# Attention blocks of 512 queries in units of two heads, with a shared bank for the block sums

## The chip, the cores and the metric

One core of one Trainium2 chip runs the whole program. The metric is the device time of one execution in microseconds (us); lower is better. The kernel before takes 1469.5 us, the median of three runs (1467.96 to 1470.09).

The engines are named as in the profile: PE is TensorE's matmul stream and PEld its weight loads, DVE is VectorE, ACT is ScalarE, POOL is GpSimd, SP starts DMAs.

## What is computed

Three layers run over x of 8 batches, 1024 tokens, 256 channels. Cut to what matters here:

```python
x = x + linear_attention(group_norm(x))      # 8 heads of 32, layer norm on q and k
t = tokens(x)
t = t + softmax_attention(layer_norm(t))     # 8 heads of 32, 1024 keys per query, then w_agg and b_agg
t = t + experts(layer_norm(t))               # Sinkhorn gates over 8 experts, top 128 tokens each, scatter back
```

The change touches the softmax attention: per batch and head, `exp(q k^T / sqrt(32))`, its sum over keys, its product with v, and the quotient.

## The kernel before, in words

Heads come in two groups (g) of four. A **unit** is one key tile of 128 keys against 256 queries for the four heads of a group. Its four score products (L894, 96 rows by 256 columns each) fill one of two score tiles `score_ps`, one ACT instruction (L1209) writes the exponentials of 128 x 1024 scores into one of four `probs` buffers, and `weigh` (L916) multiplies them by v into the lower half of the PSUM bank `acc`, each head on 32 output partitions of its own, so that the four heads run at the same time. Eight units (kt = 0 to 7) make a **block**: 256 queries of one group. A **slot** is two units; a batch has 32 slots, a block has four.

The sum over keys is split. For kt 1 to 5, DVE adds the exponentials to `prob_sum` (`add_up`, L1635), in 128 x 512 instructions, two for a unit; the first of a block adds units 0 and 1. For kt 6 and 7 PE adds them with a matrix of ones (L913) into the upper half of `acc`, and `total` (L926) adds `prob_sum` in the same way. At the end of a block ACT copies `acc` to `acc_sb` (L1199), DVE inverts the sums (`invert`, L1609) and POOL multiplies (`divide`, L1242); the result, `attn_T`, is what `agg` multiplies by w_agg.

Everything else is a list of **steps** (`order`), dealt over the slots of a batch: while batch b is in softmax attention, the front of batch b+1 (`xT`, `x_stats`, `gmean`, `gvar`, `xn`, `qk0`, `v0`, `dots`, `lin`, `zT`, `proj`, `v`, `norms`) and the store of batch b-1 (`agg`, `store_stats`, `store_rows`, `z2T`, `gate`) are worked off between the units. A `rest` in the list leaves slots empty. Within a slot every engine goes, in its own program order, through: the score products or exponentials of the next slot, the first half of the slot's steps, `weigh` or `add_up` of this slot, the second half. No engine reorders, so an instruction that waits holds all that stands behind it on its engine. PE writes the products of steps into three `shared` banks in turn, and each must be read by ACT or DVE before its next use.

Two waits matter: the score products of a unit wait until the tile's last exponentials are done (`exp_done`), and the exponentials wait until their buffer's last content has been weighed (`weighed`) and added up (`summed`). So DVE may be about one slot behind before ACT stops, and ACT about one slot before PE stops.

The routing of the experts (Sinkhorn, selection, gathers and scatters) is spread over the last three batches and a tail without attention.

## Time and profile before

| | us |
|---|---|
| median of three runs | 1469.5 |
| profiled execution, its span | 1467.7 |
| PE busy | 1339.3 (91%) |
| DVE busy | 1021.3 (70%) |
| ACT busy | 868.7 (59%) |
| POOL busy | 562.6 (38%) |

The span is the profiled execution from its first to its last instruction; the median of the runs is 1.8 us above it. Busy times are unions of an engine's records. Matmuls are pipelined, so the length of one record is more than what it costs in a stream: the distance from one start to the next is the price.

### The profile page before, as it was taken

Reading aid. Unit: us, or ns where it says so; the run is one execution under the profiler, and the core shown is the slowest. Engines: PE = TensorE matmul, PEld = TensorE weight load, DVE = VectorE, ACT = ScalarE, POOL = GpSimd, SP = SyncE. Lnnn points to the kernel's source line nnn. Section 1 sums busy time; section 2 is a strip of 40 time slices with the busy share of each in tenths; the row PEclk is TensorE's granted clock in tenths of the full one; section 3 lists DMA queues with packets and bytes.
Section 4 is the critical chain, followed back from the end, with each engine's and each line's share of the span. In section 5 each row is a group of like instructions: output and inputs, shape, how many; then the busy total and the mean of one; then the engine's idle time right before and its main releaser. Section 6 shows DMA issues by size and latency. Waiting matters only on the chain.

```text
span 1467.7 us, 29142 instructions
## 1 busy us (share of the span) xinstructions
PE 1339.3 (91%) x10849; PEld 915.8 (62%) x10849; DVE 1021.3 (70%) x2114; ACT 868.7 (59%) x1268; POOL 562.6 (38%) x1068
## 2 busy tenths in 40 slices
PE   5789989999999999999999999999998999987535
PEld 3556656667576767676767676656666567766423
DVE  3536766858585857586768676787789776899771
ACT  2456557677667767677666767665675667542100
POOL 1132530445134513551245214520554116875443
PEclk9899989999999999999999999999999999999665
DMA  2051013600360037002710272005500265454322
GB/s 79 29 137 51 1 30 87 172 16 27 80 184 15 2 93 193 18 2 75 184 46 2 57 168 79 2 30 117 144 15 2 65 169 191 128 158 134 118 68 80
DMA packets 66785, 119.13 MB, mean 81 GB/s; under 512 B 10705, under 2 KB 46546, under 8 KB 66642
## 3 DMA queue, kind: packets, MB, share of 16 engines
q1 hardware_dynamic: 57682, 90.48, 22.9%
q0 software_dynamic: 8960, 26.75, 6.0%
q8 instruction: 89, 1.46, 0.4%
q14 instruction: 54, 0.44, 0.1%
HBM read 29.11 MB, written 33.55 MB: 43 GB/s over the span
## 4 chain that ended last, share of the span: by engine, by line
PE 62%; DVE 24%; issue 6%; POOL 4%; ACT 3%; DMA 0%; DVEq 0%; POOLq 0%; ACTq 0%
PE shared L938 30%; PE scores L894 12%; PE acc L916 11%; DVE prob_sum L1635 6%; PE acc L913 3%; PE shared L933 3%; DVE acc_sb L1609 2%; DVE bn L1344 2%; ACT probs L1209 2%; DVE work L1543 1%; PE acc L926 1%; DVE resid L1350 1%; DVE best_i L1541 1%; DVE best L1539 1%; DVE bn_x L1404 1%
## 5 line engine op out<-in xcount | busy, mean ns | idle before, releaser
L1209 ACT ACTIVATE probs<-scores 128x1024 f32<-128x1024 f32 x512 | 516.0, 1024 | 178.1 <-PE scores L894 94.0
L894 PE MATMUL scores<-query_stack,key_stack 96*128 96x256 f32 x2048 | 342.1, 308 | 16.0 <-ACT probs L1209 15.7
L1635 DVE TENSOR_TENSOR prob_sum<-prob_sum,probs 128x512 f32<-128x512 f32 x512 | 331.3, 707 | 0.0
L894 PEld LDWEIGHTS scores<-query_stack,key_stack 96*128 96x128 f32 x2048 | 275.9, 192 | 85.1 <-issue 39.1
L916 PE MATMUL acc<-probs,v_all 128*32 128x256 f32 x4096 | 289.2, 389 | 0.0
L1242 POOL TENSOR_TENSOR attn_T<-acc_sb 128x256 f32<-128x256 f32 x56 | 41.4, 740 | 447.8 <-DVE acc_sb L1609 445.0
L938 PE MATMUL shared<-w_sb,chan 128*128 128x512 f32 (+1 forms) x512 | 186.7, 501 | 5.9 <-DVE chan L1438 5.9
L916 PEld LDWEIGHTS acc<-probs,v_all 128*32 128x32 f32 x4096 | 114.8, 110 | 104.0 <-issue 37.9
L938 PEld LDWEIGHTS shared<-w_sb,chan 128*128 128x128 f32 x512 | 91.9, 192 | 62.5 <-issue 57.9
L938 PE MATMUL shared<-chan,w1T 128*128 128x512 f32 x256 | 121.3, 608 | 2.1 <-ACT chan L1125 2.1
L1635 DVE TENSOR_TENSOR prob_sum<-probs 128x512 f32<-128x512 f32 x128 | 98.4, 810 | 18.8 <-ACT probs L1209 16.5
L1609 DVE RECIPROCAL acc_sb<-acc_sb 128x256 f32<-128x256 f32 x64 | 111.4, 1740 | 0.0
L1494 DVE TENSOR_TENSOR lo<-shared,hi 128x512 fp32r<-128x512 f32 x64 | 43.4, 684 | 97.2 <-ACT hi L1162 97.2
L1453 DVE TENSOR_REDUCE ss<-v_all 128x16 f32<-128x512 f32 x64 | 43.8, 685 | 77.6 <-ACT v_all L1139 77.3
L913 PE MATMUL acc<-probs,ones 128*32 128x256 f32 x1024 | 83.0, 397 | 0.0
L1132 ACT ACTIVATE lo<-shared 128x512 f32<-128x512 f32 x64 | 38.1, 595 | 70.8 <-PE shared L938 70.4
L938 PEld LDWEIGHTS shared<-chan,w1T 128*128 128x128 f32 x256 | 46.8, 193 | 50.5 <-issue 49.8
L1499 DVE TENSOR_REDUCE norm_max<-shared 128x1 f32<-128x512 f32 x64 | 43.5, 681 | 39.1 <-PE shared L938 39.1
L1162 ACT ACTIVATE hi<-shared 128x512 fp32r<-128x512 f32 x64 | 37.5, 595 | 51.8 <-PE shared L938 51.5
L787 POOL TENSOR_TENSOR lo<-lo,hr 128x512 f32<-128x512 f32 x46 | 57.1, 1264 | 20.3 <-DVE hr L1371 19.1
L938 PE MATMUL shared<-waggT,attn_T 128*128 128x256 f32 x248 | 61.7, 383 | 1.1 <-DVE attn_T L1619 1.1
L938 PE MATMUL shared<-w1T,chan 128*128 128x256 f32 x256 | 61.2, 384 | 0.0
(220 smaller groups left out, 2036.7 us busy)
## 6 DMA issues: line engine op xcount, KB each, us to landing
query_stack<-hi SPq DMA_DIRECT2D x120, 128.0 KB, 2.5
key_stack<-hi SPq DMA_DIRECT2D x120, 128.0 KB, 2.5
x_sb<-in_x_dram SPq DMA_DIRECT2D x8, 1024.0 KB, 5.3
out_dram<-resid SPq DMA_DIRECT2D x16, 512.0 KB, 4.8
tokens_scratch<-resid SPq DMA_DIRECT2D x16, 512.0 KB, 5.5
tokens_scratch<-rows SPq DMA_DIRECT2D x16, 512.0 KB, 3.3
key_stack<-lo SPq DMA_DIRECT2D x60, 128.0 KB, 2.5
query_stack<-lo SPq DMA_DIRECT2D x60, 128.0 KB, 2.5
```

Of the source, the lines that this page charges most:

```text
L787: last = eng.tensor_tensor(view, view, hr[:, t, :].unsqueeze(2).to_broadcast([P, 2 * H, DH]), ALU.mult)
L894: last = pe.matmul(score_ps[u % 2][:, QB * r:QB * (r + 1)], key_stack[stack, HG * g + r, P * kt:P * (kt + 1)], query_stack[stack, HG * g + ...
L913: pe.matmul(acc[DH * r:DH * (r + 1), QB:2 * QB], ones[:, 0:DH], p[:, QB * r:QB * (r + 1)], start=False, stop=False, skip_group_check=True, ...
L916: last = pe.matmul(acc[DH * r:DH * (r + 1), 0:QB], v_all[:, g, kt, DH * r:DH * (r + 1)], p[:, QB * r:QB * (r + 1)], start=kt == 0, stop=kt ...
L933: last = pe.transpose(ps[:, P * j:P * (j + 1)], m, ident[:, :])
L938: last = pe.matmul(out, stationary, moving, start=j == 0, stop=j == len(pairs) - 1)
L1209: act.activation(probs[:, u % PROBS, :], score_ps[u % 2][:, :], ACT.Exp, scale=DH ** -0.5) \
L1453: dve.tensor_reduce(ss[:, t, :], squares[:, t % 2, :].rearrange("p (h d) -> p h d", d=DH), AX.X, ALU.add).then_inc(s["squares_summed"], 1)
L1494: read(dve.tensor_tensor(lo[:, j, part].bitcast(F32R), ps[:, :], hi[:, j, part], ALU.subtract), seg, *st)
L1499: read(dve.tensor_reduce(norm_max[:, seg.front, j, h:h + 1], ps[:, :], AX.X, ALU.max), seg, *st)
L1609: dve.reciprocal(acc_sb[:, QB:2 * QB], acc_sb[:, QB:2 * QB]).then_inc(s["recip_ready"], 1)
L1635: dve.tensor_tensor(total[:, part], probs[:, (u - 1) % PROBS, part] if kt == 1 else total[:, part], probs[:, u % PROBS, part], ALU.add).th ...
```

## The change

QB becomes 512, so a unit is one key tile against 512 queries for **two** heads (`pair` 0 or 1), and a slot is one key tile with both pairs. A block is 512 queries of one group and has eight slots (one for each kt); a batch has four blocks and still 32 slots.

- Score products: 2 per unit over 512 columns, where there were 4 over 256. One exponential instruction still has 128 x 1024 elements.
- `weigh` and the products with ones go over 512 columns, with half as many instructions. `acc` is now full with the weighed values, so the sums go to one of the three shared banks (`bank_uses` takes it at kt 6 after the first half of the slot, and holds it until the end of kt 7). `total` stands in the slot of kt 6.
- The exponentials of kt 0 are written straight into `prob_sum`; DVE adds kt 1 to 5, two 128 x 1024 instructions for a slot, in five slots in succession. The adds of kt 1 wait for the weighing of kt 0, the exponentials of kt 0 wait for `total` of the block before.
- `copy_acc` is two ACT copies of 128 x 512 per block, of which there are half as many, `invert` is two reciprocals of 128 x 256 and stands between the halves of the slot of kt 0, no longer at its end; `divide` is two multiplications.
- In `order`, `x_stats` and `gmean` come earlier, `agg` 4 to 7 later, since their tokens belong to the last block of the batch.
- The descriptor space of the software DMA queue is set to 8192 bytes.

```diff
-QB = 256
+QB = 512
...
-             ("store_stats", 0), ("xT", 1, 1), ("xT", 0, 0), ("agg", 4), ("agg", 5), ("x_stats",), ("agg", 6),
-             ("store_rows", 0), ("rest", 1), ("agg", 7), ("gmean",), ("store_rows", 1), ("store_rows", 2),
-             ("gvar",), ("store_stats", 1), ("z2T", 0), ("store_rows", 3), ("z2T", 1), ("z2T", 2), ("z2T", 3),
+             ("store_stats", 0), ("xT", 1, 1), ("xT", 0, 0), ("x_stats",), ("store_rows", 0), ("gmean",),
+             ("store_rows", 1), ("rest", 0.5), ("agg", 4), ("agg", 5), ("agg", 6), ("gvar",), ("agg", 7),
+             ("store_rows", 2), ("store_stats", 1), ("z2T", 0), ("store_rows", 3), ("z2T", 1), ("z2T", 2), ("z2T", 3),
...
+            if kt == T - DIRECT and not second:
+                held = take((None, ("total", slot.pair // BLOCK_SLOTS)), banks)
+        if kt == T - 1:
+            held = None
...
+        return probs[:, (2 * ((T - 1) * (k // T) + kt - 1) + pair) % PROBS, :] if kt else prob_sum[:, pair, :]
...
-                for r in range(HG):
-                    last = pe.matmul(score_ps[u % 2][:, QB * r:QB * (r + 1)],
-                                     key_stack[stack, HG * g + r, P * kt:P * (kt + 1)],
-                                     query_stack[stack, HG * g + r, QB * qb:QB * (qb + 1)], start=True, stop=True)
+                for r in range(UNIT_HEADS):
+                    h = HG * g + UNIT_HEADS * pair + r
+                    last = pe.matmul(score_ps[pair][:, QB * r:QB * (r + 1)], key_stack[stack, h, P * kt:P * (kt + 1)],
+                                     query_stack[stack, h, QB * qb:QB * (qb + 1)], start=True, stop=True)
...
-                    weigh(2 * k)
-                    weigh(2 * k + 1)
-                    if k % BLOCK_PAIRS == BLOCK_PAIRS - 1:
-                        total(k // BLOCK_PAIRS)
+                    weigh(k)
+                    if k % T == added + 1:
+                        total(k // T)
...
+                if k % T == 0:
+                    await_count(act, "totalled", k // T)
+                else:
+                    n = before_in_buffer(k)
+                    if n >= 0:
+                        act.wait_ge(s["weighed"], n + 1)
+                    if n >= 0 and n % T <= added:
+                        act.wait_ge(s["summed"], 2 * (added * (n // T) + n % T - 1) + pair + 1)
...
+            def add_up(k, pair):
+
+                kt, total = k % T, prob_sum[:, pair, :]
+                dve.wait_ge(s["exp_done"], 2 * k + pair + 1)
+                if kt == 1:
+                    dve.wait_ge(s["weighed"], k)
+                else:
+                    dve.wait_ge(s["summed"], 2 * (added * (k // T) + kt - 2) + pair + 1)
+                dve.tensor_tensor(total, total, unit_probs(k, pair), ALU.add).then_inc(s["summed"], 1)
...
-                if k is not None:
-                    if k % BLOCK_PAIRS < BLOCK_PAIRS - 1:
-                        add_up(2 * k)
-                    add_up(2 * k + 1)
+                if k is not None and 1 <= k % T <= added:
+                    add_up(k, 0)
+                    add_up(k, 1)
+                elif k and k % T == 0:
+                    invert(k // T - 1)
                 for st in second:
                     step(*st)
-                if k and k % BLOCK_PAIRS == 0:
-                    invert(k // BLOCK_PAIRS - 1)
```

How the instructions stand at the head of a full batch, first on PE. The group statistics of the next batch (`gmean`, the product of `gn_mean` and `small`) wait for DVE's `mean_ready`. Before, all eight `agg` steps (two products each, `waggT,attn_T`) have gone ahead of it; these rows are of slot 3:

```order
L894 MATMUL scores<-query_stack,key_stack 128x256 [waits exp_done]
L894 MATMUL scores<-query_stack,key_stack 128x256 x3
L894 MATMUL scores<-query_stack,key_stack 128x256 [waits exp_done]
L894 MATMUL scores<-query_stack,key_stack 128x256 x3
L938 MATMUL shared<-waggT,attn_T 128x256 [waits attn_ready,read1]
L938 MATMUL shared<-waggT,attn_T 128x256
L938 MATMUL shared<-small,gn_mean 128x2 [waits mean_ready,read2]
L913 MATMUL acc<-probs,ones 32x256 [waits exp_done]
```

In the changed kernel it stands in slot 1, with `agg` 0 to 3 ahead of it, and the score products for slot 3 and then `agg` 4 to 7 behind it:

```order
L969 MATMUL shared<-ident,x_sb 128x128 [waits x_loaded,read2]
L969 MATMUL shared<-ident,x_sb 128x128 x3
L952 MATMUL acc<-probs,v_all 32x512 [waits exp_done]
L952 MATMUL acc<-probs,v_all 32x512 x3
L974 MATMUL shared<-small,gn_mean 128x2 [waits mean_ready,read0]
L922 MATMUL scores<-query_stack,key_stack 128x512 [waits exp_done]
L922 MATMUL scores<-query_stack,key_stack 128x512
L922 MATMUL scores<-query_stack,key_stack 128x512 [waits exp_done]
L922 MATMUL scores<-query_stack,key_stack 128x512
L974 MATMUL shared<-waggT,attn_T 128x256 [waits attn_ready,read1]
```

`gmean` has moved forward past `agg` 4 to 7, from slot 3 to slot 1.

On DVE, the way to `mean_ready` (the COPY into `small`, step `x_stats`) in the kernel before, from directly behind the one reciprocal of slot 0 (`acc_sb<-acc_sb`) on:

```order
L1350 TENSOR_TENSOR resid<-shared,resid 128x256
L1344 BN_STATS bn<-resid 128x6
L1350 TENSOR_TENSOR resid<-shared,resid 128x256
L1344 BN_STATS bn<-resid 128x6 x2
L1362 BN_AGGR mv<-bn 128x2 x4
L1404 BN_STATS bn_x<-chan 128x6
L1635 TENSOR_TENSOR prob_sum<-prob_sum,probs 128x512 x4
L1404 BN_STATS bn_x<-chan 128x6
L1350 TENSOR_TENSOR resid<-shared,resid 128x256 x2
L1344 BN_STATS bn<-resid 128x6
L1409 BN_AGGR mv_x<-bn_x 128x2 x2
L1411 COPY small<-mv_x 128x2
```

That is slots 0 to 2; the same way in the changed kernel, slots 0 and 1, from the reciprocals on:

```order
L1654 RECIPROCAL acc_sb<-acc_sb 128x256 x2
L1393 TENSOR_TENSOR resid<-shared,resid 128x256 x2
L1387 BN_STATS bn<-resid 128x6
L1393 TENSOR_TENSOR resid<-shared,resid 128x256
L1387 BN_STATS bn<-resid 128x6
L1393 TENSOR_TENSOR resid<-shared,resid 128x256
L1387 BN_STATS bn<-resid 128x6 x2
L1405 BN_AGGR mv<-bn 128x2 x4
L1447 BN_STATS bn_x<-chan 128x6 x2
L1678 TENSOR_TENSOR prob_sum<-prob_sum,probs 128x1024 x2
L1452 BN_AGGR mv_x<-bn_x 128x2 x2
L1454 COPY small<-mv_x 128x2
```

A second reciprocal and, of the same two slots, only one round of adds (1024 wide, kt 1) stand ahead of the copy now, and both reciprocals stand ahead of the first additions of `agg` (`resid<-shared,resid`); those of `agg` 4 and 5 no longer stand ahead of the copy.

The third place is DVE from `gvar` to the adds behind `xn` 0 (`chan<-chan,small`), slots 3 to 5 in the kernel before:

```order
L1433 TENSOR_SCALAR small<-shared 128x2
L1344 BN_STATS bn<-resid 128x6
L1362 BN_AGGR mv<-bn 128x2 x4
L1635 TENSOR_TENSOR prob_sum<-probs 128x512 x2
L1438 TENSOR_SCALAR chan<-chan,small 128x512 x2
L1400 TENSOR_SCALAR gates<-shared 128x8
L1609 RECIPROCAL acc_sb<-acc_sb 128x256
L1635 TENSOR_TENSOR prob_sum<-prob_sum,probs 128x512 x4
```

And in the changed kernel:

```order
L1476 TENSOR_SCALAR small<-shared 128x2
L1393 TENSOR_TENSOR resid<-shared,resid 128x256
L1387 BN_STATS bn<-resid 128x6 x2
L1405 BN_AGGR mv<-bn 128x2 x4
L1678 TENSOR_TENSOR prob_sum<-prob_sum,probs 128x1024 x2
L1481 TENSOR_SCALAR chan<-chan,small 128x512 x2
L1443 TENSOR_SCALAR gates<-shared 128x8
L1678 TENSOR_TENSOR prob_sum<-prob_sum,probs 128x1024 x4
```

Where two 512-wide adds stood ahead of `xn` 0 and four behind it after a reciprocal, two 1024-wide ones (kt 3) stand ahead and four (kt 4 and 5) directly behind.

## Rows read from the trace of the kernel before

**Rows 1.** The page: busy time by engine, and the last-ending chain by engine.

```profile
PE 1339.3 (91%) x10849; PEld 915.8 (62%) x10849; DVE 1021.3 (70%) x2114; ACT 868.7 (59%) x1268; POOL 562.6 (38%) x1068
...
PE 62%; DVE 24%; issue 6%; POOL 4%; ACT 3%; DMA 0%; DVEq 0%; POOLq 0%; ACTq 0%
```

**Rows 2.** Busy times in windows: batches 2, 5, 6, 7; last PEclk, DMA.

```profile
411.30:561.30 150.00, 149.32 (x1301) 101.45 (x1297) 103.79 (x194) 104.83 (x152) 55.71 (x125) 1.00 0.28 75
...
861.20:1021.40 160.20, 155.85 (x1316) 104.60 (x1312) 123.48 (x241) 104.97 (x152) 55.42 (x125) 0.99 0.27 70
1021.40:1185.60 164.20, 155.64 (x1310) 105.77 (x1306) 134.47 (x284) 105.85 (x154) 63.24 (x125) 0.98 0.24 62
1185.60:1336.00 150.40, 139.88 (x1294) 103.59 (x1291) 124.88 (x285) 84.86 (x116) 97.55 (x111) 0.97 0.54 161
```

**Rows 3.** The costliest groups of the page (busy, mean ns of one, idle before).

```profile
L1209 ACT ACTIVATE probs<-scores 128x1024 f32<-128x1024 f32 x512 | 516.0, 1024 | 178.1 <-PE scores L894 94.0
L894 PE MATMUL scores<-query_stack,key_stack 96*128 96x256 f32 x2048 | 342.1, 308 | 16.0 <-ACT probs L1209 15.7
...
L1609 DVE RECIPROCAL acc_sb<-acc_sb 128x256 f32<-128x256 f32 x64 | 111.4, 1740 | 0.0
```

**Rows 4.** PE in order of time at the head of batch 2 (start, us).

```profile
411.30 1.21 PE L894 MATMUL scores<-query_stack,key_stack 96*128 96x256 f32 x8
...
415.96 1.31 PE L894 MATMUL scores<-query_stack,key_stack 96*128 96x256 f32 x8
417.11 1.89 PE L938 MATMUL shared<-waggT,attn_T 128*128 128x256 f32 x8
...
425.50 1.21 PE L894 MATMUL scores<-query_stack,key_stack 96*128 96x256 f32 x8
426.55 1.03 PE L938 MATMUL shared<-waggT,attn_T 128*128 128x256 f32 x4
427.41 0.28 PE L938 MATMUL shared<-small,gn_mean 128*128 128x2 f32 x2
...
428.94 0.61 PE L916 MATMUL acc<-probs,v_all 128*32 128x256 f32 x8
429.37 0.61 PE L926 MATMUL acc<-prob_sum,ones 128*32 128x256 f32 x8
...
437.39 1.88 PE L938 MATMUL shared<-w_sb,chan 128*128 128x512 f32 x4
```

**Rows 5.** PE around one fp32r product over 512 columns.

```profile
226.80 0.40 PE L938 MATMUL shared<-norm_sq,head_ones 128*128 128x512 f32 x1
227.03 0.60 PE L933 MATMUL shared<-ident,rows 128*128 128x128 f32 x4
```

**Rows 6.** DVE in order of time in the same stretch.

```profile
414.82 1.27 DVE L1635 TENSOR_TENSOR prob_sum<-probs 128x512 f32<-128x512 f32 x2
...
417.02 1.74 DVE L1609 RECIPROCAL acc_sb<-acc_sb 128x256 f32<-128x256 f32 x1
418.68 0.36 DVE L1350 TENSOR_TENSOR resid<-shared,resid 128x256 f32<-128x256 f32 x1
...
421.26 2.48 DVE L1635 TENSOR_TENSOR prob_sum<-prob_sum,probs 128x512 f32<-128x512 f32 x4
...
424.26 0.73 DVE L1350 TENSOR_TENSOR resid<-shared,resid 128x256 f32<-128x256 f32 x2
...
425.54 0.17 DVE L1411 COPY small<-mv_x 128x2 f32<-128x2 f32 x1
...
430.62 0.16 DVE L1433 TENSOR_SCALAR small<-shared 128x2 f32<-128x2 f32 x1 [0.54 <-PE shared L938]
...
435.32 1.00 DVE L1438 TENSOR_SCALAR chan<-chan,small 128x512 f32<-128x512 f32 x2 [2.61 <-POOLq L1268]
```

**Rows 7.** PE after the `dots` products (weigh, then `lin` 0).

```profile
495.47 1.07 PE L916 MATMUL acc<-probs,v_all 128*32 128x256 f32 x16
496.75 0.68 PE L938 MATMUL shared<-hi 128*128 128x128 f32 x4 [0.21 <-DVE hi L1478]
```

**Rows 8.** Windows of 4 us where PE waited, and behind (columns as Rows 2).

```profile
168.00:172.00 4.00, 1.63 (x21) 0.88 (x14) 4.00 (x5) 2.56 (x3) 3.22 (x3) 0.88 0.00 0
172.00:176.00 4.00, 4.00 (x29) 2.65 (x33) 3.39 (x6) 2.31 (x3) 0.00 (x0) 0.50 0.01 4
```

More of the change, by code:

```diff
@@ L1613, in invert @@
-                if g == 0:
-                    storing = next(seg for seg in segments if seg.has("store") and seg.stores == a - 1)
-                    for t in range(QB // P * qb, QB // P * (qb + 1)):
-                        await_read(dve, storing, "agg", t)
-                dve.wait_ge(s["recip_ready"], blk + 1)
-                dve.wait_ge(s["attn_ready"], blk)
-                dve.tensor_tensor(attn_T[:, g, QB * qb:QB * (qb + 1)], acc_sb[:, 0:QB], acc_sb[:, QB:2 * QB],
-                                  ALU.mult).then_inc(s["attn_ready"], 1)
@@ L1622, in add_up @@
[L1622 to L1636 removed]
+                a, g, qb = blk // BLOCKS, blk % BLOCKS // NQB, blk % NQB
@@ new lines, in invert @@
+                dve.wait_ge(s["acc_copied"], blk + 1)
+                for h in range(2):
+                    part, tokens = slice(HALF * h, HALF * (h + 1)), QB * qb + HALF * h
+                    if g == 0:
+                        storing = next(seg for seg in segments if seg.has("store") and seg.stores == a - 1)
+                        for t in range(tokens // P, (tokens + HALF) // P):
+                            await_read(dve, storing, "agg", t)
+                    dve.wait_ge(s["recip_ready"], 2 * blk + h + 1)
+                    dve.wait_ge(s["attn_ready"], 2 * blk + h)
+                    dve.tensor_tensor(attn_T[:, g, tokens:tokens + HALF], acc_sb[:, 0, part], acc_sb[:, 1, part],
+                                      ALU.mult).then_inc(s["attn_ready"], 1)
```

194 lines of the change are left out of this document (104 added, 90 removed).

## The prediction

> **What bounds the kernel now.** I read the page first: PE is busy 91% and has 62% of the chain that ended last, DVE 24% of it [rows 1]. Then the batches one by one. In batch 2, 149.3 of 150.0 us are PE's at full clock, while DVE and ACT have 104 and 105 [rows 2]: for batches 1 to 4 PE's instruction stream is the time, and every other engine is hidden. Batches 5 and 6 carry Sinkhorn and selection on DVE (123 and 134 us) and take 160 and 164; PE has a little room there. In batch 7 no engine is full by itself. So a saving on PE counts in full in batches 1 to 4, unless another engine comes to stand in PE's way; and since no engine reorders, that is decided where PE waits for DVE.
>
> **What the wide products save.** Eight score products cost 1.05 us from their first start to the next instruction's (425.50 to 426.55), and 1.15 where a plain product runs ahead, whose end hides about 0.19 of it (415.96 to 417.11) [rows 4]: about 0.12 each, 0.96 to 1.05 for a slot. An fp32r product over 512 columns does occur: 0.23 us from its start to the next one's [rows 5]. The lower bound is half of a two-pass fp32 product over 512 columns, four passes in about 1.72 (record 1.88, less the tail), 0.43 each, so 0.215 [rows 4]. Four of them are 0.86 to 0.94. I take a saving of 0.10 for a slot (bounds 0.02 and 0.19), 3.2 us for a batch, 26 for 256 slots.
>
> The Trainium skill says otherwise, in "TensorE: Matmul & The Clock Gate", section "Wait — 56ns, not 53.3ns?": back-to-back products start N/2.4 + 2.5 ns apart, so width alone would change almost nothing. By that page a slot would go from 0.87 to 0.86 and the whole gain would be an estimated 2 us. The trace disagrees at 256 columns (0.12, not 0.109) [rows 4].
>
> `weigh`, ones and `total` keep their columns. Eight records (four heads at once, two passes) take 0.43 for 256 columns [rows 4], half as many over 512 take the same per column. Nothing saved, nothing lost. ACT has the same 512 exponentials of 1.02 us [rows 3] and the same number of copies; in slots without steps they, at 2.05, now set the pace against PE's 1.95: nothing more than PE's saving there is lost.
>
> **DVE's work.** Four 512-wide adds take 2.48 and two 1.27, so they start 0.60 apart and one record is 0.67; a 256-wide addition is 0.36 [rows 6], so 256 elements are worth 0.27 to 0.30. A 1024-wide add is then 0.54 more than a 512-wide one, 1.14 (upper bound two narrow ones, 1.20; lower bound 0.60, if width cost nothing, which the 256-wide row excludes), 2.3 for a slot. The total falls a little (320 x 1.14 against 640 x 0.60, 20 us off the critical path). What changes is where it lies: 2.3 in each of five slots in succession, where it was 1.2, 2.4, 2.4, 0. The reciprocals keep their number, two of 1.66 (417.02 to 418.68) [rows 6], but stand back to back and ahead of the slot's second half.
>
> **The head of a batch.** I walk it with slot 0's first score product at 0 (411.30 before). Before, `mean_ready` comes at 14.4 (425.54 + 0.17) and PE gets to `gmean` at 16.1 [rows 4, 6]: no wait. In the new order DVE has, ahead of that copy, one more reciprocal (+1.7) and a start 0.4 later (ACT makes two copies of the block first), but the two adds of slot 0 (-1.2) and `agg` 4 and 5 with statistics (424.26 to about 425.25, -1.0) are gone, and the adds of slot 1 are 0.2 shorter: 14.1 [rows 6]. PE gets there at about 10.6: slot 0 is 4.5, then scores 0.9, `agg` 2 and 3 1.7 [rows 4], a wait of 1.2 for the bank that `agg` 0 fills (its DVE read stands behind both reciprocals, at 7.6), transposes and `weigh` 2.0. PE then waits 3.5 us at `gmean`, with the next scores and `agg` 4 to 7 queued behind.
>
> DVE goes on: scores and `agg` 4 (PE) make it 16.2; `agg` 4 and 5 on DVE 17.8; adds of kt 2 20.1; `agg` 6 and `gvar` 20.9; `agg` 7 and statistics 22.4; adds of kt 3 24.7; `xn` 0 must wait for POOL's root, 4.7 after `gvar` as before (430.62 to 435.32) [rows 6], 25.5; `xn` and a gate 26.5; adds of kt 4 28.8. The exponentials of kt 6 use the buffers of kt 4, so they end at 29.8, and the score products behind them at 30.3. That is where the first `qk0` product starts, at 26.1 before (437.39) [rows 4]. Without waits PE would be there at 24.2: 26.1, less 1.3 for one block's ones and total, which now come later (three groups of 0.43 [rows 4]), less 0.6 of scores. **The head costs 6.1 us of waits.**
>
> **Later in a batch.** (a) `lin` 0 now directly follows `dots`, without `weigh` between. Before, PE went on 1.28 us after `dots` (495.47 to 496.75), with 0.21 of real wait [rows 7]; now all of it is a wait: +1.0. (b) `qT` of the second half stands one slot earlier, while DVE's and POOL's scaling, just in time before, needs the same time: +0.4. (c) kt 1 to 5 of the third block fall on slots 17 to 21, of which 19 to 21 are nearly empty: PE needs 2.0 there, DVE 2.3 plus statistics. Counting DVE from `dots` on gives the adds of kt 3 at 11.7 and so the scores of slot 22 at 13.3, against 11.9 for PE alone: with 0.3 at slot 20, +1.7. Together 3.1. In the projections (slots 24 to 29) PE's slots are 6 us and hide DVE. The held bank meets almost no steps (three in slots 6 and 7, none at the other three block ends of a full batch): nothing; uncovered, each would cost an ACT read of about 0.6.
>
> **Clock.** Waits of this size have a second price. In 168 to 172 PE was busy 1.6 of 4 us, and in the next 4 us its granted clock was 0.50, that is 1.2 GHz [rows 8]: 2 us of work given away. In the new head one such drop may follow `gmean` (DVE is the bound there, so it hides) and one the waits of slots 5 and 6. I take 1 us for a batch, bounds 0 and 5.
>
> **The sum.** A full batch: -3.2 + 6.1 + 3.1 + 1.0 = +7.0; four of them +28. Batches 5 and 6 have the same head, but later DVE's extra work already sets the pace: +4 each, +8. Batch 0 has no `agg`, so no long DVE chain at the head: +1. Batch 7: gain and longer DVE bursts cancel, 0. The end: the last block is now needed for `agg` 4 to 7, and behind it stand one more copy and one more reciprocal of 1.7 [rows 3]: +2. The smaller descriptor space has no row that prices it; I take 0, and if it bound it would cost some us in the last batch and the tail, which the range holds. That is +39 on the profiled 1467.7, 1506.7; the median of the runs lies 1.8 above the span: **1508 us**.
>
> **The rivals.**
> - Forecast, waits outweigh the products: 60%, 1508, own range 1485 to 1528.
> - *The products are worth what their busy row says.* L894 shows 342.1 us busy for 2048 [rows 3]; if 1024 wide ones take 0.235 each, 241, the gain is 101 instead of 26 and the time 1434, **faster**. For it: weight loads halve. Against: the distance between starts, not the record, is the price, and it is 0.12. It decides from about 0.25 us for a slot (65 us of losses over 256). 17%, with all smaller mixtures that end faster.
> - *The clock falls twice in every batch* after the two long waits, at 2.9 us each: 35 more, about 1540. For it: rows 8, where waits like those of slots 5 and 6 did it. Against: at the head PE's slowness is partly hidden behind DVE. 13%.
> - *Only the wait at `gmean` comes*, and DVE catches up in the empty slots 4 and 5: the head costs about 3.5, the rest nothing, so about 0 for a batch and 1470 to 1475. Against: adds of 2.3 in slots of 2.0. 10%, half of it within what can be told from no change.
>
> About 0.2% (3 us) is what a measurement of this kernel can tell. Faster 17%, same 5%, slower 78%. The range 1470 to 1540 takes in all but the second rival and the top of the third.
>
> **What would show it.** Right: a wait of PE's `gmean` for DVE's `small` of 3 to 4 us in each batch; ACT exponentials waiting for `prob_sum` adds in slots 4 to 6 and 20 to 22, the score products behind them; batches of about 157 us where they were 150; score groups at 0.86 to 0.94. Each is a step: groups above 0.94 or below 0.86 break the first, a short wait at `gmean` the head, 1024-wide adds well below 1.1 the chain, PEclk below 1 behind the waits the clock term. Wrong it would be above all if DVE were earlier at `mean_ready` than I count, since both the head's wait and its tail hang on that one chain.

## The result and the profile after

The changed kernel takes **1560.36 us** (median of 4 runs, 1558.96 to 1562.3), the kernel before beside it 1469.26 (1467.96 to 1470.09): ratio 1.0626, 95% interval 1.0611 to 1.0641. That is 91 us slower. The direction was forecast, the size was not: 1508 us lay 52 us below, and the range ended at 1540.

From the page of the changed kernel, the engines' busy times, as in [rows 1]:

```profile
PE 1357.2 (87%) x7009; PEld 759.3 (49%) x7009; DVE 989.6 (64%) x1794; ACT 873.3 (56%) x1268; POOL 614.8 (39%) x1068
```

PE is busy 18 us longer with fewer instructions, and idle 72 us more of a span that grew by 89.7 (1557.4 against 1467.7). DVE is busy 32 us less: DVE's total is no bound. POOL is busy 52 us more with the same 1068 instructions. That was in no term of the forecast, and it is the first thing to ask about.

The windows of the changed kernel by batch (busy time of PE, PEld, DVE, ACT, POOL, then the granted clock and DMA), batches 0, 1, 4, 5, 6, 7 and the end, as in [rows 2]:

```profile
97.80:257.90 160.10, 145.38 (x750) 71.71 (x748) 95.79 (x130) 103.91 (x145) 49.77 (x91) 0.98 0.21 50
257.90:420.60 162.70, 152.67 (x820) 82.75 (x816) 100.21 (x154) 105.88 (x152) 64.16 (x125) 0.98 0.26 69
...
748.10:910.80 162.70, 153.23 (x820) 82.77 (x816) 100.19 (x154) 105.89 (x152) 64.00 (x125) 0.98 0.26 69
910.80:1082.10 171.30, 157.70 (x836) 85.20 (x832) 120.30 (x203) 105.93 (x152) 63.37 (x125) 0.98 0.24 65
1082.10:1254.70 172.60, 155.86 (x831) 84.44 (x827) 131.94 (x241) 106.32 (x153) 69.10 (x125) 0.97 0.22 59
1254.70:1417.20 162.50, 142.03 (x812) 83.60 (x808) 119.69 (x243) 84.09 (x115) 97.65 (x112) 0.93 0.50 149
1417.20:1557.40 140.20, 72.49 (x273) 55.16 (x265) 82.77 (x245) 14.98 (x31) 56.44 (x58) 0.65 0.30 94
```

Against the same stretches of before (batch 0 163.8; batches 1 to 4 150.0, 150.0, 149.9, 150.0; batch 5 160.2; batch 6 164.2; batch 7 to its last `weigh` 148.7; the end 133.4), the forecast and what came:

| part | forecast | measured |
|---|---|---|
| batch 0 | +1 | -3.7 |
| batches 1 to 4 | +28 | +53.0 |
| batches 5 and 6 | +8 | +19.5 |
| batch 7 | 0 | +13.8 |
| the end | +2 | +6.8 |
| ahead of batch 0 | 0 | +0.3 |
| sum | +39 | +89.7 |

**The head of a batch.** PE of the changed kernel in order of time, batch 4, whose slot 0 starts at 748.07 (answers to [rows 4]):

```profile
748.07 1.19 PE L922 MATMUL scores<-query_stack,key_stack 96*128 96x512 f32 x4
...
755.61 1.13 PE L974 MATMUL shared<-waggT,attn_T 128*128 128x256 f32 x4 [0.76 <-DVE resid L1393]
...
762.25 0.56 PE L974 MATMUL shared<-small,gn_mean 128*128 128x2 f32 x2 [3.63 <-DVE small L1454]
762.67 2.05 PE L922 MATMUL scores<-query_stack,key_stack 96*128 96x512 f32 x4
764.52 3.62 PE L974 MATMUL shared<-waggT,attn_T 128*128 128x256 f32 x8
768.07 1.45 PE L952 MATMUL acc<-probs,v_all 128*32 128x512 f32 x8
...
780.75 0.73 PE L922 MATMUL scores<-query_stack,key_stack 96*128 96x512 f32 x2 [0.85 <-ACT probs L1249]
781.88 0.73 PE L922 MATMUL scores<-query_stack,key_stack 96*128 96x512 f32 x2 [0.40 <-ACT probs L1249]
782.46 1.88 PE L974 MATMUL shared<-w_sb,chan 128*128 128x512 f32 x4
```

The wait at `gmean` is 3.63 us, where 3.5 was forecast. What follows was missed: four score products take 1.85 us to the next start (764.52 less 762.67) and eight records of `agg` 3.55, where 1.0 and 1.8 are usual (the same two in the run with the wait filled, below). The first `qk0` product comes 34.4 us after the batch's start, where 30.3 was forecast and 26.1 was before: the head loses 8.3 us and not 4.2.

**POOL.** The same head, POOL of the changed kernel (the row deviations, operations of 4 columns):

```profile
759.52 2.24 POOL L338 TENSOR_SCALAR ln_h<-ln_h 128x4 f32<-128x4 f32 x1
761.84 0.20 POOL L339 TENSOR_TENSOR ln_r<-ln_r,ln_h 128x4 f32<-128x4 f32 x1
...
778.49 4.54 POOL L336 TENSOR_TENSOR ln_h<-ln_r 128x4 f32<-128x4 f32 x1
```

and DVE beside it:

```profile
759.37 2.34 DVE L1678 TENSOR_TENSOR prob_sum<-prob_sum,probs 128x1024 f32<-128x1024 f32 x2
761.63 0.27 DVE L1452 BATCH_NORM_AGGREGATE mv_x<-bn_x 128x2 f32<-128x12 f32 x2
761.93 0.17 DVE L1454 COPY small<-mv_x 128x2 f32<-128x2 f32 x1
...
766.47 0.42 DVE L1393 TENSOR_TENSOR resid<-shared,resid 128x256 f32<-128x256 f32 x1 [2.88 <-PE shared L974]
768.17 0.43 DVE L1393 TENSOR_TENSOR resid<-shared,resid 128x256 f32<-128x256 f32 x1 [1.28 <-PE shared L974]
...
778.34 4.62 DVE L1678 TENSOR_TENSOR prob_sum<-prob_sum,probs 128x1024 f32<-128x1024 f32 x4
```

An operation that takes 0.20 us alone takes 2.24 and 4.54 while two or four adds run one behind the other (759.37 to 761.7, 778.34 to 783.0). The copy that is `mean_ready` (761.93) stands behind two of them, and the two `resid` rows wait for PE, which will matter below.

**Batch 7**, where nothing was forecast. PE of the changed kernel, slots 4 and 5, and ACT:

```profile
1270.64 0.82 PE L922 MATMUL scores<-query_stack,key_stack 96*128 96x512 f32 x2
1277.91 1.22 PE L922 MATMUL scores<-query_stack,key_stack 96*128 96x512 f32 x2 [6.45 <-ACT probs L1249]
1278.93 1.91 PE L974 MATMUL shared<-waggT,attn_T 128*128 128x256 f32 x4
```

```profile
1268.98 1.02 ACT L1249 ACTIVATE probs<-scores 128x1024 f32<-128x1024 f32 x1 [0.83 <-PE scores L922]
1275.86 1.09 ACT L1139 ACTIVATE rows<-resid,ln_b,ln_r 128x256 f32<-128x256 f32 x2 [5.85 <-POOLq L1299]
1276.85 1.91 ACT L1249 ACTIVATE probs<-scores 128x1024 f32<-128x1024 f32 x2
```

PE stands 6.45 us for an exponential. ACT had its score products at 1271.5; it stood at `store_rows` 0 (L1139) for POOL's row deviations, 5.85 us, with that exponential behind it. The order had moved `store_rows` 0 and 1 of batch 7 from slots 6 and 7 to slot 4, in front of `agg` 4.

### The profile page after: what moved, and what is told of

It reads as the page before. It is cut to its first block and busy times, and to the rows that moved or that the text cites. A ratio compares the mean times of both kernels' runs of the same rounds, so it can differ in the third digit from the quotient of the medians.

```text
span 1557.4 us, 21137 instructions
## 1 busy us (share of the span) xinstructions
PE 1357.2 (87%) x7009; PEld 759.3 (49%) x7009; DVE 989.6 (64%) x1794; ACT 873.3 (56%) x1268; POOL 614.8 (39%) x1068
## 5 line engine op out<-in xcount | busy, mean ns | idle before, releaser
L1249 ACT ACTIVATE probs<-scores 128x1024 f32<-128x1024 f32 x448 | 451.4, 1024 | 135.4 <-PE scores L922 76.5
L1678 DVE TENSOR_TENSOR prob_sum<-prob_sum,probs 128x1024 f32<-128x1024 f32 x320 | 391.5, 1267 | 0.0
L922 PE MATMUL scores<-query_stack,key_stack 96*128 96x512 f32 x1024 | 334.7, 443 | 37.5 <-ACT probs L1249 36.2
L922 PEld LDWEIGHTS scores<-query_stack,key_stack 96*128 96x128 f32 x1024 | 181.1, 193 | 181.3 <-ACT probs L1249 96.1
L952 PE MATMUL acc<-probs,v_all 128*32 128x512 f32 x1792 | 242.8, 614 | 0.0
L952 PEld LDWEIGHTS acc<-probs,v_all 128*32 128x32 f32 x1792 | 42.4, 110 | 99.1 <-issue 89.4
L1249 ACT ACTIVATE prob_sum<-scores 128x1024 f32<-128x1024 f32 x64 | 63.5, 1020 | 37.0 <-PE scores L922 36.9
L946 PE MATMUL shared<-probs,ones 128*32 128x512 f32 x512 | 69.1, 611 | 5.9 <-DVE v_all L1622 3.4
L1139 ACT ACTIVATE rows<-resid,ln_b,ln_r 128x256 f32<-128x256 f32 x64 | 37.5, 597 | 61.1 <-POOLq L1299 52.0
L1296 POOL TENSOR_SCALAR ln_v<-mv 128x4 f32<-128x4 f32 x28 | 16.9, 604 | 133.3 <-DVE mv L1405 132.1
```

The source lines that it names most:

```text
L922: last = pe.matmul(score_ps[pair][:, QB * r:QB * (r + 1)], key_stack[stack, h, P * kt:P * (kt + 1)], query_stack[stack, h, QB * qb:QB * (q ...
L946: last = pe.matmul(ps[DH * r:DH * (r + 1), :], ones[:, 0:DH], head_probs(k, r), start=kt == added + 1, stop=kt == T - 1, skip_group_check= ...
L952: last = pe.matmul(acc_ps[DH * r:DH * (r + 1), :], v_all[:, g, kt, DH * r:DH * (r + 1)], head_probs(k, r), start=kt == 0, stop=kt == T - 1 ...
L1249: act.activation(unit_probs(k, pair), score_ps[pair][:, :], ACT.Exp, scale=DH ** -0.5) \
L1678: dve.tensor_tensor(total, total, unit_probs(k, pair), ALU.add).then_inc(s["summed"], 1)
```

## Experiments

All times are medians of 4 runs; the kernel before, run beside each group, had 1467.6, 1466.7, 1469.3, 1466.4 and 1465.0. So the groups lie up to 4 us apart by themselves: the ratios take this out, but a difference of some us between runs of different groups is not told apart by the medians alone. Slots are counted from the first score product that PE issues in them.

**Places of single steps, and the products.** `gmean` later, with `gvar` behind `store_stats` 1:

```diff
-("x_stats",), ("store_rows", 0), ("gmean",), ("store_rows", 1), ("rest", 0.5),
-("agg", 4), ("agg", 5), ("agg", 6), ("gvar",), ("agg", 7), ("store_rows", 2), ...
+("x_stats",), ("store_rows", 0), ("store_rows", 1), ("rest", 0.5), ("agg", 4),
+("agg", 5), ("agg", 6), ("gmean",), ("agg", 7), ("store_rows", 2),
+("store_stats", 1), ("z2T", 0), ("store_rows", 3), ("gvar",), ...
```

> The changed kernel with one line of the order altered: the product `gmean` stands behind `agg` 6 (slot 3) and not in slot 1, `gvar` behind `store_rows` 3. Theory A (the loss is PE's wait at `gmean`, 3.6 us for a batch, and the about 4 us by which the work behind it runs long while TensorE's granted clock is at the lower of its two levels): six batches give back 5 to 7.5 us each, 30 to 45 us, so 1515 to 1530 us. Rival B (DVE's chain is the bound in the head, PE only waits elsewhere): at most 10 us back, 1550 to 1560.

Measured: 1613.44 us, ratio 1.1002 (1.0959 to 1.1045): 53 us slower than the changed kernel. A miss on the other side. PE and ACT in batch 4:

```profile
788.32 1.13 PE L974 MATMUL shared<-waggT,attn_T 128*128 128x256 f32 x4
794.58 2.13 PE L922 MATMUL scores<-query_stack,key_stack 96*128 96x512 f32 x4 [5.13 <-ACT probs L1249]
...
813.68 2.36 PE L922 MATMUL scores<-query_stack,key_stack 96*128 96x512 f32 x4 [5.92 <-ACT probs L1249]
```

```profile
792.52 1.09 ACT L1139 ACTIVATE rows<-resid,ln_b,ln_r 128x256 f32<-128x256 f32 x2 [7.16 <-POOLq L1299]
```

The wait did not go, it changed its place: ACT stands 7.16 us at `store_rows` 0 (still in slot 1), and PE behind ACT. The second wait has another cause in the same edit: `store_stats` 1 now stands ahead of `gvar`, so POOL works out the row deviations first, `xn` comes late, and DVE's adds and the exponentials wait behind it. The edit moved two things, and says nothing against the wait at `gmean`.

The wait filled, not removed:

```diff
 elif kind == "gmean":
+    for n in range(16):
+        pe.matmul(ps[:, 0:P], ones[:, :], ones[:, :], start=True, stop=True)
     pe.wait_ge(s["mean_ready"], seg.fronts + 1)
```

> The changed kernel with 16 products of 128x128 (about 3.4 us, results overwritten) issued by PE ahead of its wait at `gmean`: the wait is filled and not removed. Theory A (the lower clock behind the wait is paid in full): the four us behind the wait run at the full clock again, 3 to 4 us for each of six batches, 18 to 24 us, so 1536 to 1542 us. Rival B (as forecast: DVE is late there anyway and hides the slow clock): no change, 1557 to 1563.

Measured: 1548.58 us, 1.0556 (1.0515 to 1.0597), 12 us less, between the two theories. Batches 1 to 4 take 159.8, 159.9, 160.1 and 159.9 where they took 162.7, 164.6, 162.9 and 162.7; `gmean` itself comes no earlier (14.2 us after the batch's start in both), so what they give back is the clock's alone. Batch 0, where PE waits only 1.52 us at `gmean` and the filling takes 3.7, takes 4.7 more. PE of that run:

```profile
753.77 3.84 PE L1002 MATMUL shared<-ones 128*128 128x128 f32 x32
757.44 0.32 PE L974 MATMUL shared<-small,gn_mean 128*128 128x2 f32 x2
757.63 1.17 PE L922 MATMUL scores<-query_stack,key_stack 96*128 96x512 f32 x4
758.64 1.89 PE L974 MATMUL shared<-waggT,attn_T 128*128 128x256 f32 x8
```

The same eight `agg` records: 1.82 us instead of 3.55. The granted clock of the two (the third number from the end) in 4 us from about the end of the wait on, first the changed kernel, then the filled one:

```profile
762.00:766.00 4.00, 3.75 (x10) 3.13 (x11) 0.74 (x5) 0.96 (x2) 2.07 (x11) 0.51 0.89 252
```

```profile
757.00:761.00 4.00, 4.00 (x28) 2.94 (x26) 1.83 (x10) 0.77 (x2) 2.20 (x11) 1.00 0.89 243
```

0.51 and 1.00, which is the lower level, 1.2 GHz, and the upper, 2.4. The slow clock costs 2.8 us in three of these batches (4.7 in batch 2), in full, not hidden behind DVE.

`store_rows` 0 and 1 of batch 7 behind all `agg`:

```diff
+    if store and not front:
+        first = [("store_rows", 0), ("store_rows", 1)]
+        steps = [x for x in steps if x not in first]
+        at = steps.index(("store_rows", 2))
+        steps[at:at] = first
     return steps
```

> The changed kernel with `store_rows` 0 and 1 of batch 7 behind all eight `agg` (slot 7 in place of 4). Theory A (ACT waits there for POOL with the exponentials of the slot behind it, so PE stands 6.5 us and then runs at the lower clock): 8 to 11 us back, 1549 to 1553 us, and the long slot 5 of batch 7 (12.0 us) falls to 4 to 5. Rival B (batch 7 is long because DVE's adds lie between routing work): within 2 us of the changed kernel, 1558 to 1562.

Measured: 1551.34 us, 1.0575 (1.0534 to 1.0617), 9.0 less. Slots 0 to 30 of batch 7 take 138.6 in sum, 148.0 in the changed kernel, 136.5 before. Theory A holds.

The wide products undone:

```diff
-last = pe.matmul(score_ps[pair][:, QB * r:QB * (r + 1)], ...)
+for c in range(2):
+    at = HALF * c
+    last = pe.matmul(score_ps[pair][:, QB * r + at:QB * r + at + HALF], ...)
```

> The changed kernel with each score product of 512 columns issued as two of 256 (same banks, same exponentials). This undoes the wide products alone. Theory A (0.92 us for four wide products against about 1.0 for eight narrow ones): plus 0.08 to 0.10 us for a slot where PE sets the time, 15 to 26 us, 1575 to 1586. Rival B (width alone changes nothing, only columns count): plus 2, 1562. Rival C (the busy row is the price): plus 60 to 100 us.

Measured: 1565.66 us, 1.0674 (1.0632 to 1.0715): **5.3 us** more (7 by the ratios), not 26 and not 60. Narrow products here start 0.118 to 0.120 apart, wide ones in the changed kernel 0.231 (median of the 418 distances under 0.25): eight and four of them differ by 0.02 to 0.04 us, 5 to 9 over 256 slots.

**Order and units apart.** `x_stats`, `gmean` and `store_rows` 0 moved ahead of `agg` 4 in the kernel before, `gmean` into slot 1:

```diff
-("agg", 4), ("agg", 5), ("x_stats",), ("agg", 6), ("store_rows", 0), ("rest", 1), ("agg", 7), ("gmean",), ("store_rows", 1), ...
+("x_stats",), ("store_rows", 0), ("gmean",), ("agg", 4), ("agg", 5), ("agg", 6), ("rest", 1), ("agg", 7), ("store_rows", 1), ...
```

> The kernel before with one line of the order altered: `gmean` in slot 1, ahead of `agg` 4 to 7, nothing else of the change. Theory A (an early `gmean` by itself makes a wait and a stretch at the lower clock): DVE's mean comes 1 to 2 us earlier than before the move, PE 5 us earlier, so a wait of 3 to 4 us and 2 to 4 us of slow clock in each of six batches: 30 to 45 us more, 1500 to 1515. Rival B (only together with the wide adds does it cost): within 8 us of before, up to 1477.

Measured: 1514.66 us, 1.0338 (1.0298 to 1.0378), 48 more than before, with no wide unit in it. Its PE:

```profile
743.36 0.56 PE L938 MATMUL shared<-small,gn_mean 128*128 128x2 f32 x2 [4.01 <-DVE small L1411]
743.77 2.05 PE L938 MATMUL shared<-waggT,attn_T 128*128 128x256 f32 x4
745.27 2.27 PE L894 MATMUL scores<-query_stack,key_stack 96*128 96x256 f32 x8
```

Wait and slow clock as in the changed kernel; batches 1 to 4 take 156.2 to 156.9.

The whole new order in the kernel before, and the whole old order in the changed kernel (nothing but the list `steps` is exchanged, by the lines of the change's own diff: applied in the first, taken back in the second):

```diff
-    steps = [("rest", 0.5), ("xT", 1, 0), ...]   # the kernel's own list
+    steps = [("rest", 0.5), ("xT", 1, 0), ...]   # the other kernel's list
```

> The kernel before with the whole order of the changed kernel (all its moves of steps, none of its units, adds, banks). Theory A (order is most of the loss): at least the cost of the early `gmean`, 1500 to 1520. Rival B (the loss is in the wide adds and the held bank): 1470 to 1480.

Measured: 1553.75 us, 1.0602 (1.0557 to 1.0646): 87 more than before, far more than theory A gave. A full batch takes 164 us there, no less than in the changed kernel.

> The changed kernel with the whole order of before (`agg` 4 and 5 in slot 1, `gmean` in slot 3). Theory A: no wait of 3.6 at `gmean`; but `agg` 4 and 5 need the last block of the batch before, whose reciprocals and product end later now, so a wait of 1 to 3 us at `agg` 4; in sum 15 to 35 us less than the changed kernel, 1525 to 1545. Rival B (the new order is the better one for the new units): 1560 or more.

Measured: 1508.08 us, 1.0287 (1.0244 to 1.0329): 41 more than before, 52 less than the changed kernel. So the order alone costs 87, the units alone 41, both 91: under the new order the units cost hardly anything more. That both spend the same slack is my reading of it. With the units alone a full batch takes 5 to 9 us more than before, 4 to 7 of them in slots 1 to 6 and 2.5 or more in slots 17 to 22; which part of the new units does it was not taken apart.

`lin` 0 one slot behind `dots`:

```diff
-("dots",), ("lin", 0), ("qT", 0, 1), ("lin", 1), ("lin", 2), ("lin", 3), ("rest", 1), ("front_stats", 0), ("rest", 2.25),
+("dots",), ("rest", 1.25), ("lin", 0), ("qT", 0, 1), ("lin", 1), ("lin", 2), ("lin", 3), ("front_stats", 0), ("rest", 2),
```

> The changed kernel with `lin` 0 one slot behind `dots` again, so that ones and weigh lie between. Forecast of the working: 1.0 us for a batch of the seven, 7 us back, 1553. Rival: the wait moves to slots 20 to 22, where DVE's adds set the pace: 0 to 2 us, 1558 to 1561.

Measured: 1561.78 us, 1.0647 (1.0597 to 1.0697): no difference in all. In its profile slots 17 to 22 take 24.6 instead of 25.7, the 1.0 of the forecast; but slots 1 to 6, which the edit does not touch, take 38.4 to 38.6 in all four full batches, where the changed kernel has that in batch 2 alone (else 36.7 to 36.9). The difference is the clock at slot 6 (0.85 and 0.72 in two windows of 4 us of batch 3, where the changed kernel has 1.00; see the last section). So the 1.0 of the forecast is there, but this run can't price it.

**DVE's adds.** Over 128 of 1024 columns, the rest of the running sum left out:

```diff
-dve.tensor_tensor(total, total, unit_probs(k, pair), ALU.add)
+dve.tensor_tensor(total[:, 0:128], total[:, 0:128], unit_probs(k, pair)[:, 0:128], ALU.add)
```

> The changed kernel with DVE's adds over 128 of the 1024 columns (an eighth of the running sum; the rest of it is left out). Theory C, formed from the traces of the first eight runs (DVE's wide adds keep POOL's operations of 4 columns waiting, so that its chain for the row deviations ends late, ACT waits for it at `store_rows` 0 and PE behind ACT): the chain of 16 operations on POOL falls from 6.6 to 4.4 us, the wait at `gmean` from 3.6 to about 1.5, the waits of slots 5, 6 and 20 to 22 go: 6 to 9 us for a batch, 1505 to 1520 us. Rival A (the places of the steps alone): at most 3 us for a batch, 1540 or more.

Measured: 1478.4 us, 1.0075 (1.0054 to 1.0096): 82 less, more than either theory gave. `gmean` waits 1.77, POOL's 16 operations take 4.65 us in place of 6.5, a full batch 154.5 to 155.8, still 4.5 or more over the 150 of before. Windows of one:

```profile
562.20:716.80 154.60, 149.56 (x812) 81.70 (x812) 63.32 (x154) 104.00 (x152) 42.54 (x125) 0.99 0.27 72
```

DVE has 37 us less (63.3 against 100.2) and POOL, whose work is the same, 21 less (42.5 against 64.0).

Each add as two of 512:

```diff
+for h in range(2):
+    part = slice(BANK * h, BANK * (h + 1))
+    last = dve.tensor_tensor(total[:, part], total[:, part], unit_probs(k, pair)[:, part], ALU.add)
+last.then_inc(s["summed"], 1)
```

> The changed kernel with each add of 1024 columns issued as two of 512, as wide as before the change. DVE's time in all is a little longer (4 x 0.60 for a slot against 2 x 1.14). If it matters to POOL how long one add holds it off: an operation of POOL that meets adds takes 0.5 and not 1.1 to 2.3 us, its chain ends up to 1 us sooner, 0 to 6 us less in all, 1554 to 1560. If only the total counts: 0 to 4 us more, 1560 to 1564.

Measured: 1564.95 us, 1.0658 (1.064 to 1.0676), 4.6 more. DVE is busy 1023.0 us in place of 989.6 and POOL 587.8 in place of 614.8: what POOL gains by it buys no time, so the length of a single add is not what costs.

`store_rows` 0 and 1 behind `agg` 7 in every batch:

```diff
-("x_stats",), ("store_rows", 0), ("gmean",), ("store_rows", 1), ("rest", 0.5), ..., ("agg", 7), ("store_rows", 2),
+("x_stats",), ("gmean",), ("rest", 0.5), ..., ("agg", 7), ("store_rows", 0), ("store_rows", 1), ("store_rows", 2),
```

> The changed kernel with `store_rows` 0 and 1 behind `agg` 7 in every batch (slot 3 in place of 1, in batch 7 slot 7), `gmean` left where it is. ACT's wait of 5.8 us for POOL in slot 1 then lies behind the exponentials of slots 2 and 3. If ACT's wait is what holds the head (theory C): slots 2 and 3 shorter by 2 to 3 us in six batches and 9 us in batch 7, 1531 to 1541. If PE's own wait at `gmean` with the clock is all (theory A): only batch 7's 9 us, 1549 to 1553.

Measured: 1551.69 us, 1.0564 (1.0546 to 1.0582): batch 7's 9 us, nothing in the others (slots 1 to 6 35.7 to 37.2). While PE waits at `gmean`, ACT's wait at `store_rows` 0 costs nothing. My theory C was wrong in this: POOL's late chain is the next wait, not the first.

The old order with `store_rows` 0 to 3 behind `gmean`, `gvar` late and `xn` 0 in slot 5:

```diff
-("store_rows", 0), ("rest", 1), ("agg", 7), ("gmean",), ("store_rows", 1), ("store_rows", 2), ("gvar",), ("store_stats", 1), ("z2T", 0), ("store_rows", 3), ..., ("xn", 0), ("gate", 0), ("rest", 2),
+("rest", 1), ("agg", 7), ("gmean",), ("store_rows", 0), ("store_rows", 1), ("store_rows", 2), ("z2T", 0), ("store_rows", 3), ("gvar",), ("store_stats", 1), ..., ("gate", 0), ("rest", 1.0), ("xn", 0), ("rest", 1.0),
```

> The changed kernel with the order of before, but `store_rows` 0 to 3 behind `gmean` in slot 3, `gvar` and `store_stats` 1 at the end of slot 3 and `xn` 0 in slot 5. Against the run with the order of before alone (1508): ACT's wait of 3.5 us for POOL in slot 2, PE's of 1.1 at `gvar` and 1.2 at slot 4's scores should go, 2 to 4 us for each of six batches, 1484 to 1496. If POOL's root for `xn` is then late (it starts at the end of slot 3), the gain is lost at `qk0` and it is 1505 to 1515.

Measured: 1517.11 us, 1.0329 (1.0312 to 1.0346), 9 more than the old order as it was (6 by the ratios). The head is a little shorter (slots 1 to 6 30.1 to 31.7, where the old order had 30.1 to 32.6), but batch 7 takes 12 more: there `store_stats` 1 now stands half a slot later, and ACT waits 6.64 us at a `store_rows` for POOL (PE 5.26 behind it), the same trap a third time.

**What makes the wait at `gmean`.** The adds of key tile 1 at the end of their slot, behind `x_stats`, in all blocks; then with `store_rows` late as well; then in slot 1 of a batch alone:

```diff
-if k is not None and 1 <= k % T <= added:
+if k is not None and 1 <= k % T <= added and k % SLOTS not in (1,):   # last run; before: 2 <= k % T
     add_up(k, 0)
     add_up(k, 1)
 ...
 for st in second:
     step(*st)
+if k is not None and k % SLOTS in (1,):                               # before: k % T == 1
+    add_up(k, 0)
+    add_up(k, 1)
```

> The changed kernel with DVE's two adds of key tile 1 at the end of their slot, behind `x_stats` and not ahead of it. Theory C' (the wait at `gmean` is made by the wide adds that stand ahead of the mean on DVE): `mean_ready` comes 2.3 us sooner, PE waits 1.3 us and not 3.6, and as it stands so briefly its clock may stay up: 2.3 to 6 us for each of six batches, 1525 to 1547 us. Rival D (ACT, at `store_rows` 0 for POOL's chain, holds slot 2 anyway): PE then stands at slot 2's scores or later instead, 1552 to 1560.

Measured: 1610.37 us, 1.0986 (1.0965 to 1.1006), 50 more than the changed kernel, which neither theory had. `gmean` waits 1.50 and slots 1 to 6 take 33.8 to 35.0 instead of 36.7 to 38.6; but slot 26 takes 11.2 to 12.8 instead of 6.9 in each full batch: there the late adds hold up exponentials (ACT waits 2.64 for them in batch 3), and PE stands behind ACT.

> The run before it with `store_rows` 0 and 1 behind `agg` 7 as well, so that neither PE's nor ACT's wait stands in slot 1. If each of the two waits covers for the other (rival D), the two edits together give more than the sum of either alone: 4 to 7 us for each of six batches and 9 in batch 7, 1508 to 1527. If they add up simply: the gain of the run before it and 9 us more, nothing beyond.

Measured: 1596.48 us, 1.0885 (1.0864 to 1.0905): 14 less than the run before it. The two profiled executions are 9.5 apart, 7.7 of it in batch 7 (slot 5 3.8 instead of 11.3); slots 1 to 6 of batch 3 take 33.8, and took 34.2. So in the profile the two edits add up simply; the rest of the 14 is not placed, and the total carries the loss of slot 26 in both.

> The changed kernel with the two adds at the end of the slot in slot 1 of each batch alone, not in the three other blocks. In the run with all four blocks the first seven slots of a batch were 2.8 us shorter (slot 1 7.6 us, slot 2 6.9, slot 5 3.2) and the loss lay elsewhere (slots 13, 16, 26). If that reading holds: 2.8 us less for each of six batches, 1541 to 1546 us, and `gmean` waits 1.5 us and not 3.6. If the gain of the head was bound to the other blocks: no change, 1557 to 1563.

Measured: 1552.74 us, 1.0592 (1.056 to 1.0623), 7.6 less than the changed kernel (5 by the ratios); 14 to 19 were expected. PE of batch 3:

```profile
598.54 0.35 PE L974 MATMUL shared<-small,gn_mean 128*128 128x2 f32 x2 [1.50 <-DVE small L1454]
598.75 1.31 PE L922 MATMUL scores<-query_stack,key_stack 96*128 96x512 f32 x4
599.86 3.47 PE L974 MATMUL shared<-waggT,attn_T 128*128 128x256 f32 x8
```

The wait is 1.50 as expected: the two wide adds ahead of the mean make 2.1 of its 3.6 us. Batches 1 to 4 give back 2.0, 2.2, 2.8 and 2.8, batches 5 and 6 0.2 and 1.9, batch 0 loses 4.3. The slow clock stays: `agg` takes 3.39 us after a wait of 1.50 too.

**How far the new units go.** The old order, `store_rows` 0 behind `gmean` in full batches; then also the last blocks divided half by half; then also the adds of slot 3 last:

```diff
+    if front and attend and store:
+        steps.remove(("store_rows", 0))
+        steps.insert(steps.index(("gmean",)) + 1, ("store_rows", 0))
```

> The changed kernel with the order of before, and `store_rows` 0 behind `gmean` (slot 3 in place of 2), all else left. ACT waited 3.5 us there for POOL with the exponentials behind it; PE then 1.2 us at slot 4's scores and a weigh at the lower clock. Gone: 1.5 to 3 us for each of six batches, 1490 to 1500 us. If POOL's chain is late for `gvar` and `xn` instead: 1503 to 1510.

Measured: 1504.08 us, 1.0253 (1.0236 to 1.0271), 4 less than the old order alone; the two intervals overlap, so the gain is not shown.

```diff
-for h in range(2): reciprocal(h)                # in short, not the kernel's own lines
-for h in range(2): product(h)
+for h in range(2): reciprocal(h); product(h)    # the last batch's blocks alone
```

> The run before it with the last batch's blocks divided in turns (reciprocal of a half, product of that half, then the second half; before both reciprocals stand ahead of both products). The tail's wait at `agg` 4 falls from 5.1 to 3.4 us, one reciprocal of 1.7 less: 1 to 2 us less than the run before it. If something later in the tail sets the end: no difference.

Measured: 1501.42 us, 1.0233 (1.0215 to 1.025), 2.7 less. The tail's wait at `agg` 4 falls from 5.06 to 3.63.

```diff
-if k is not None and 1 <= k % T <= added:
+if k is not None and 1 <= k % T <= added and k % SLOTS not in (3,):
 ...
+if k is not None and k % SLOTS in (3,):   # behind the slot's second half
+    add_up(k, 0)
+    add_up(k, 1)
```

> The best version so far (order of before, `store_rows` 0 behind `gmean`, last blocks divided in turns: 1501) with DVE's two adds of slot 3 at the end of the slot, behind `gvar` and the statistics. POOL's root for `xn` starts 1.5 to 2.3 us sooner, and PE's wait of 1.2 at `qk0` with the slow stretch behind it goes: 1 to 2 us for each of six batches, 1489 to 1496. If exponentials then wait for the adds instead: 1500 or more. It is not expected to reach the 1466 to 1469 of before.

Measured: 1499.48 us, 1.0242 (1.0217 to 1.0267), full batches 154.9 to 155.6. The wait of 1.24 at `qk0` falls to 0.63 or goes; one of 1.01 for transposed rows comes in slot 4. By the ratios this run is no better than the one before it. The two are the best versions run, 34 and 35 us above their kernels before. None beats it.

## Why the forecast was wrong in size

**The products, the first term, failed.** The forecast had 0.10 us saved for a slot, 26 in all; undoing them costs 5.3, 0.02 for a slot, the lower of its own bounds. The step that failed is the comparison of groups: 0.96 to 1.05 for eight narrow products held, with them, the end of a group that a wide one has too, while 4 x 0.215 to 0.235 had none. Measured alike, from first start to the next product of another kind behind a plain one, medians are 1.146 before (one of them is the 1.15 in [rows 4]) and 1.121 after. The Trainium skill ("TensorE: Matmul & The Clock Gate", "Wait — 56ns, not 53.3ns?") had the size nearly right: its 2.5 ns for each product gave an estimated 2 us (1024 products fewer make it an estimated 2.6). Its spacing is still low here, 0.109 against 0.118 to 0.120, and 0.216 against 0.231. The rival of the busy row fell: that row fell from 342.1 to 334.7 us only. This term accounts for 2.5 us of the 5.7 by which a full batch was missed (12.7 in batch 4, not 7.0; the four together missed 6.2 each, with a second fall of the clock in batch 2).

**The wait at `gmean` was right**: 3.6 against 3.5, 0.76 against 1.2 at `agg` 3, `mean_ready` at 14.0 against 14.1, adds at 1.14.

**The clock term failed.** The forecast took 1 us for a batch on the ground that DVE was the bound behind `gmean` and would hide PE's slow stretch. DVE was waiting for PE there: its `resid` rows above wait 2.88 and 1.28 us for PE's `agg`. Filling the wait gives 2.8 us back. That is 1.9 of the miss; the rival with two drops of 2.9 in a batch was nearer than the forecast itself, though only the first comes each time.

**The other waits of a full batch** were undersized by 1.3 us: three chains meet in the head (DVE's mean, POOL's row deviations, POOL's root for `xn`), and POOL's were taken at their old length.

**Batch 7 at 0 was wrong**, and not for its size: `store_rows` ahead of `agg` 4 was in the order that I had before me, and I did not ask who waits behind ACT. It cost 9.0 of 13.8 us by experiment. The rest is not settled.

**The end**: the forecast's mechanism (a second reciprocal of 1.7 ahead of the last products) was right, its size not: the wait is 5.06 where it was 1.12, and the four records behind it take 1.84 to the next start, where 0.94 was usual. PE of the changed kernel:

```profile
1423.39 2.04 PE L974 MATMUL shared<-waggT,attn_T 128*128 128x256 f32 x4 [5.06 <-DVE attn_T L1667]
```

Dividing in turns took 1.4 off the wait. The smaller descriptor space, which the forecast had at 0, shows in no row: PE waits 12.8 us for DMA in all, 12.7 before, and the gathers of the software queue land in a median of 3.5 to 3.6 us, 3.6 to 3.8 before. It was not run alone. **Batch 0** gained 3.7 where +1 stood, and not at its head: there the forecast saw no long chain, but PE waits 1.52 at `gmean` and 3.07 at `qk0`, and slots 1 to 6 take 32.4 where they took 27.6. The gain lies in slots 19 and 23 (3.2 and 6.5 where they took 5.7 and 11.1), and its cause stays open.

In sum: 21 us of the 51 that were missed in the profile are the products that gave 5 and not 26; some 12 the clock in six batches; 9 batch 7; 5 the end; 8 the other waits, which nothing here tells apart further; and batch 0 with the rest of batches 2 and 7 takes 4 off. Where the loss itself comes from is shown from both sides: the order alone brings 87 of it with the old units, and shorter adds take 82 away under the new order (how much they would take from the old one was not tried, but in batches 1 to 4 PE was busy 149.3 of 150.0 us there [rows 2], which leaves them little to take). The reading that fits both: PE, ACT and POOL are brought early to steps whose inputs DVE makes, and DVE's adds stand ahead of them.

## What to carry to other kernels

When a change moves steps, walk every engine's queue at each moved step, and not only the one that was the bound: write down who waits there, for whom, and what stands behind. A wait that another one covers costs nothing as long as it is covered (moving ACT's alone gave nothing in a full batch); take away the first and PE stands at the second, so try each edit alone and then both. And compare two groups of products from the same mark to the same mark, for a saving of some hundredths times hundreds of slots lives in that difference.
